# GpSimd normalises the keys by adding a negative mean instead of subtracting the mean

## The reference

```
norm_X   = layernorm(ctx, norm1_w, norm1_b)          # the keys, and the values
norm_F_L = layernorm(x + tgt2, norm2_w, norm2_b)     # the queries
attended = softmax(norm_F_L @ norm_X.T / 16) @ norm_X
h        = gelu(attended @ fc1_w.T + fc1_b)          # 4 columns
cross    = h @ fc2_w.T + fc2_b
norm_c   = layernorm(cross, norm3_w, norm3_b)
out      = norm_F_L + gamma2 * (cross + gamma1 * softmax(norm_c @ norm_c.T / 16) @ norm_c)
```

## Time and profile before

| | us |
|---|---|
| median of 3 runs | 325.54 (324.9 to 326.22) |
| the profiled execution, its own time | 324.85 |
| its span | 323.1 |

### The profile page before, as it was taken

The page is one execution under the profiler, slowest core; times in us unless marked ns, Lnnn a source line. Parts: engine busy times, 40 slices in busy tenths (PEclk is TensorE's granted clock), DMA queues, the critical chain, the costliest instruction groups (busy, mean ns, idle before and its releaser), DMA issues.

```text
span 323.1 us, 4581 instructions
## 1 busy us (share of the span) xinstructions
PE 236.0 (73%) x1614; PEld 151.0 (47%) x1614; DVE 200.4 (62%) x377; ACT 140.9 (44%) x265; POOL 157.6 (49%) x141
## 2 busy tenths in 40 slices
PE   5789971398898797878988799300678888773990
PEld 4665640377676595656767597100223222221330
DVE  6585744689765595766576433399444444427992
ACT  1253831158656375656557484400353443321220
POOL 8000199959999999999999920007000000000000
PEclk9956998589999799999999999955555555555555
DMA  7910000074314243432400000000000000000998
GB/s 234 388 63 2 1 3 1 0 231 156 134 40 144 78 133 130 132 131 78 149 35 2 1 2 0 0 0 0 2 1 0 2 0 0 2 0 1 359 365 318
DMA packets 14710, 26.79 MB, mean 83 GB/s; under 512 B 1760, under 2 KB 1760, under 8 KB 14688
## 3 DMA queue, kind: packets, MB, share of 16 engines
q1 hardware_dynamic: 14688, 26.50, 23.6%
HBM read 18.11 MB, written 8.39 MB: 82 GB/s over the span
## 4 chain that ended last, share of the span: by engine, by line
POOL 40%; PE 30%; DVE 20%; issue 4%; ACT 3%; DMA 1%; SPq 0%; DVEq 0%; ACTq 0%; POOLq 0%
POOL cN L586 23%; POOL xN L567 10%; POOL rstd L574 6%; DVE Fall L530 6%; DVE nm L485 5%; PE psum L960 5%; PE psum L833 4%; PE psum L930 3%; PE psum L790 3%; PE psum L802 2%; PE psum L779 2%; PE psum L749 2%; PE psum L813 2%; PE psum L968 1%; DVE PT L457 1%
## 5 line engine op out<-in xcount | busy, mean ns | idle before, releaser
L586 POOL TENSOR_SCALAR cN<-cN,bn,rstd 128x256 f32<-128x256 f32 x64 | 80.0, 1259 | 1.5
L833 PE MATMUL psum<-XT,Fall 128*128 128x256 f32 x256 | 62.9, 390 | 0.0
L833 PEld LDWEIGHTS psum<-XT,Fall 128*128 128x128 f32 x256 | 48.0, 198 | 5.6
L317 DVE BATCH_NORM_STATS2 bn<-xN 128x6 f32<-128x512 f32 x32 | 22.3, 699 | 28.0 <-POOL xN L567 28.0
L567 POOL TENSOR_TENSOR xN<-xN,tgt 128x512 f32<-128x512 f32 x30 | 38.1, 1274 | 1.9 <-DMA xN<-x 1.9
L682 ACT ACTIVATE PT<-psum 128x512 f32<-128x512 f32 x32 | 19.1, 597 | 43.3 <-PE psum L841 43.3
L410 DVE TENSOR_REDUCE nmax<-psum 128x2 f32<-128x512 f32 x32 | 22.0, 688 | 21.8 <-PE psum L833 21.8
L779 PE MATMUL psum<-ident,cN 128*128 128x128 f32 x128 | 20.2, 290 | 17.3 <-POOL cN L586 17.3
L333 DVE TENSOR_SCALAR xN<-xN,bn,rstd 128x256 f32<-128x256 f32 x64 | 30.0, 512 | 0.1
L669 ACT ACTIVATE Fall<-psum,par 128x512 f32<-128x512 f32 x32 | 23.4, 791 | 13.6 <-PE psum L779 13.5
L688 ACT ACTIVATE E<-psum,nmax 128x256 f32<-128x256 f32 x64 | 26.7, 471 | 5.8 <-DVE nmax L410 5.8
(11 more groups left out here) (153 smaller groups left out, 340.3 us busy)
## 6 DMA issues: line engine op xcount, KB each, us to landing
cN<-ctx SPq DMA_DIRECT2D x32, 256.0 KB, 3.0
xN<-x SPq DMA_DIRECT2D x32, 256.0 KB, 4.1
out<-Fall SPq DMA_DIRECT2D x32, 256.0 KB, 3.5
x0T<-x0t SPq DMA_DIRECT2D x1, 256.0 KB, 2.8
wqT<-wqt SPq DMA_DIRECT2D x1, 256.0 KB, 3.0
c0T<-c0t SPq DMA_DIRECT2D x1, 256.0 KB, 3.5
wkT<-wkt SPq DMA_DIRECT2D x1, 256.0 KB, 4.6
wvT<-wvt SPq DMA_DIRECT2D x1, 256.0 KB, 4.9
```

Of the source, the lines that this page charges most:

```text
L317: dve.bn_stats(bn[:, (b // 2) % 4, side, b % 2, :], src[:, b % SLOTS, :].rearrange("p (t d) -> p d t", t=NT)).then_inc(st_ok, 1)
L586: pool.tensor_scalar(own, own, stat(p, 0, m, t, 1), root_of(p, 0, m, t), ALU.subtract, ALU.mult)\
L833: last = pe.matmul(bank[SBANK1[b % 3]][:, t * N:(t + 1) * N], Fall[:, b, c, t * P:(t + 1) * P], XT[:, p % 4, c, m * N:(m + 1) * N], start= ...
```

## The change

The negative means are written to a new small array `nmean`. VectorE writes them with one more `tensor_scalar` ahead of the one that writes the variances: once for the first three pairs (12 columns), and once for each of the 13 later pairs (4 columns). GpSimd's `tensor_scalar` of L586 keeps its tile, its shape and its number, but its two operations are add and mult where they were subtract and mult, and its first pointer leads to `nmean` in place of `bn`. GpSimd has one more wait in `normal` for each batch of the later pairs. VectorE's own `normal` (L333) keeps subtract and mult.

```diff
+    nmean = sb("nmean", [P, 4, 2 * NT])
...
         def variances(p):
             sides = slice(1, 2) if p < EARLY else slice(0, 2)
             dve.wait_ge(st_ok, stats[0])
+            if p >= EARLY:
+                dve.tensor_scalar(nmean[:, p % 4, :].rearrange("p (m t) -> p m t", t=NT),
+                                  bn[:, p % 4, 0, :, :].rearrange("p m (t k) -> p m t k", t=NT)[:, :, :, 1],
+                                  -1.0, None, ALU.mult).then_inc(nmean_ok, 1)
             dve.tensor_scalar(vps[:, p % 4, sides, :]...
...
                 elif p == 2 * EARLY:
                     dve.wait_ge(st_ok, 2 * EARLY)
+                    dve.tensor_scalar(nmean[:, 0:EARLY, :].rearrange("p q (m t) -> p q m t", t=NT),
+                                      bn[:, 0:EARLY, 0, :, :].rearrange("p q m (t k) -> p q m t k", t=NT)[:, :, :, :, 1],
+                                      -1.0, None, ALU.mult).then_inc(vps_first, 1)
...
             if p < EARLY:
                 pool.wait_ge(root_first, 1)
             else:
+                pool.wait_ge(nmean_ok, p - EARLY + 1)
                 pool.wait_ge(root_ok, p + 1)
             for t in range(NT):
                 own = cN[:, b % SLOTS, t * D:(t + 1) * D]
-                pool.tensor_scalar(own, own, stat(p, 0, m, t, 1), root_of(p, 0, m, t), ALU.subtract, ALU.mult)\
+                pool.tensor_scalar(own, own, nmean[:, p % 4, NT * m + t:NT * m + t + 1], root_of(p, 0, m, t), ALU.add,
+                                   ALU.mult)\
                     .then_inc(zc_ok, 1)

         pool.wait_ge(consts, 13)
-        pool.wait_ge(vps_first, 1)
+        pool.wait_ge(vps_first, 2)
```

More of the change, by code:

```diff
@@ L173, in build @@
     y_first, y_ok, st_ok = sem("y_first"), sem("y_ok"), sem("st_ok")
-    vps_first, vps_ok, root_first, root_ok = sem("vps_first"), sem("vps_ok"), sem("root_first"), sem("root_ok")
+    nmean_ok, vps_first, vps_ok, root_first, root_ok = sem("nmean_ok"), sem("vps_first"), sem("vps_ok"), sem("root_first"), sem("root_ok")
     zc_ok, zy_ok, t_mm, evac_ok = sem("zc_ok"), sem("zy_ok"), sem("t_mm"), sem("evac_ok")
```

## The result

The changed kernel takes 297.77 us (median; 295.92 to 298.40), the kernel before 325.22 us beside it (321.41 to 326.22): a ratio of 0.9166, with a 95% interval of 0.9081 to 0.9252. The forecast was faster, 304.5 us, with a range from 302.5 up. The way is right, and the gain is larger than the range allowed. The profiled execution takes 298.40 us with a span of 296.5, against 324.85 and 323.1 before.

What follows compares the result with a forecast made beforehand. GpSimd was taken as the bound, with TensorE waiting for its normalised `cN`. Loop -16.3, first stretch -4.9, late root +0.2 gave -21.0 us, so 304.5 us; range 302.5 to 326.5.

Steps and rivals of the forecast that it cites:

- The price of the instruction: GpSimd's L586, 64 times: from 1219 ns undisturbed to 0.60 us, taken from the two-input add and subtract per element.
- The loop: From 72 to 182 us, TensorE's whole 17.3 us of waits for `cN` goes and no more; gain 16.3 us.
- the 1.0 us kept back: In the loop, an allowance of 1.0 us for new waits, such as a late maximum on VectorE.
- My window for the 7.83: One pair's period of the loop, 9.20 us long, in which TensorE was busy 7.83 us, taken as its need.
- the threshold: In the loop, GpSimd stops being the bound at (7.83 - 4.21) / 4 = 0.90 us per L586 instruction.
- The first stretch: From 41 to 61 us, twelve L586 instructions fall from 15.0 to 7.2 us; VectorE normalises earlier; gain 4.9 us.
- The collision that I had put into the range: First stretch: GpSimd's add beside VectorE's adds might cost 0.56 us; two such collisions cut the gain to 3.6 us.
- The clock behind the pause: TensorE restarts at half clock after its pause, before as after the change; costs and gives nothing.
- VectorE's instructions and GpSimd's wait: VectorE's 14 new instructions hidden in the loop, 0.4 us if GpSimd stays the bound; added wait nothing to some hundredths each.
- my bound of 0.48: Upper cost of one added VectorE instruction, from its twin L324, which ranges from 169 to 480 ns.
- rival A: In L586, add and mult cost the same as subtract and mult: 0.4 us added, 325.9 us; chance 0.31.
- +0.2: The one late root, at 72.06 us, which waits for its variances behind VectorE's new instruction: 0.2 us lost.

Runs made afterwards that it cites:

- run 1: The kernel before with only subtract changed to add in GpSimd's normalising, the pointer still leading to the statistics: 296.61 us, ratio 0.918.
- run 7: The changed kernel plus 16 GpSimd `tensor_scalar` probes of operation pairs on a scratch array before its first root: 0.56 or 1.22 us each at 256 elements.
- 3: The changed kernel with subtract and the old pointer kept for the first 12 normalisings (first three pairs), add for the others: 305.21 us.
- run 9: The changed kernel with VectorE's negative means counted into `vps_ok`, so GpSimd has one wait instead of two: 297.81 us.
- Run 10: run 9 with GpSimd's first add made to wait until VectorE has done its own two adds of `tgt2`: 296.37 us, ratio 0.9139.
- 12: The changed kernel with subtract kept in 1 of 4 normalisings: 298.67 us, ratio 0.9194.
- run 6: The changed kernel with 60 transposes of a constant filling TensorE's pause before the first xN transposes: 297.56 us, ratio 0.9186.
- 11: The changed kernel with subtract kept in 3 of 8 normalisings: 302.57 us, ratio 0.9314.
- run 2: The changed kernel with the mean written with its own sign and subtract kept, new array and added waits included: 327.12 us, ratio 1.0073.
- run 8: run 2 with VectorE's means counted into `vps_ok`, so GpSimd has one wait instead of two: 324.88 us, ratio 1.0004.

## Why the prediction was right and wrong

*The price of the instruction.* Right in its place and near in size: 0.60 us taken, 0.554 median. The reasoning held in what decides (the data are not the limit of this form, and its price can hang on its operations), and run 1 shows that nothing else matters. The way to 0.60 was luck: I scaled the two-input add, and the quick form is in truth 0.34 us and 0.83 ns per element, the rate at which two of the casts grow, (825 - 507) / 384 for L624 and L620. The GPSIMD Engine Reference of the Trainium skill (section 3.1) gives 1.03 cycles per element for a loop of at most two operations, an estimated 0.86 ns at its 1.2 GHz. That agrees with the quick pairs of run 7, and not with the others, at 3.5 ns.

*The loop: the step that failed.* I took 7.83 us of busy time as TensorE's need in a period, wrote that "the whole 17.3 us of TensorE's wait goes and no more", and kept 1.0 us of that back: 16.3. Measured: 21.4. The waits did go whole. The words "and no more" failed, because TensorE's busy time shrank as well. From its second score to its last product with `V1` (columns as in the earlier trace rows), before and after:

```profile
68.93:205.02 136.09, 116.70 (x872) 92.45 (x871) 86.21 (x181) 83.39 (x154) 116.01 (x89) 0.99 0.26 86
```

```profile
63.97:178.66 114.69, 112.59 (x873) 91.39 (x871) 89.12 (x194) 81.37 (x154) 81.10 (x89) 1.00 0.32 106
```

For the same instructions TensorE is busy 4.1 us less (116.70 - 112.59) and idle 17.3 us less (19.39 - 2.10). Two things make up the 4.1 us, and a third is the 1.0 us kept back.

First, a group of transposes that is cut by the wait counts as more busy time than a whole one. TensorE in order of time, one pair of the kernel before, and then the same group after:

```profile
133.78 0.38 PE L779 MATMUL psum<-ident,cN 128*128 128x128 f32 x2
135.53 0.88 PE L779 MATMUL psum<-ident,cN 128*128 128x128 f32 x6 [1.37 <-POOL cN L586]
136.25 1.89 PE L833 MATMUL psum<-XT,Fall 128*128 128x256 f32 x8
```

```profile
118.10 1.04 PE L789 MATMUL psum<-ident,cN 128*128 128x128 f32 x8
118.97 1.89 PE L843 MATMUL psum<-XT,Fall 128*128 128x256 f32 x8
```

From the first transpose to the score it is 2.47 us before, of which 1.37 is shown as a wait, and 0.87 us after. The difference is 1.60, so 0.23 us more goes than the wait. All 11 waits cut their group in the same way, into two and six, so over 11 that is 2.5 us.

Second, TensorE's clock fell once inside the loop of the kernel before, and not after. A window of each time, before, and one group in it:

```profile
108.00:110.00 2.00, 2.00 (x10) 1.73 (x9) 1.13 (x2) 1.47 (x2) 2.00 (x2) 0.55 0.00 0
110.00:112.00 2.00, 2.00 (x8) 1.57 (x6) 0.00 (x0) 0.00 (x0) 1.90 (x3) 0.59 0.00 0
```

```profile
108.66 3.36 PE L833 MATMUL psum<-XT,Fall 128*128 128x256 f32 x8
```

This score takes 3.36 us, the others 1.89, and the six transposes ahead of it 1.13 in place of 0.88: 1.7 us of busy time that hid a wait. The next pair, at about 117 us, is the one that has no wait for `cN`: 12 pairs, 11 waits. Before the fall TensorE had waited 1.75 us for `cN`, no longer than in other periods, where the clock stayed; what set it off isn't shown. 17.3 + 2.5 + 1.7 = 21.5, against 21.4 measured. Third, the 1.0 us that I kept back for new waits did not come: the loop takes 114.69 or 114.70 us in every run in which GpSimd is quick enough (after, 1, 3, 7, 9, 10 and 12), and 114.78 in run 6.

My window for the 7.83 was also unlucky. Pairs alternate between 7.64 and 7.20 us after (from the starts of the scores at 111.33, 118.97 and 126.17 us), and it lay on the longer kind. Runs 11 and 12 show what this means for the threshold: it is (7.42 - 4.21) / 4 = 0.80 us, not 0.90, or 0.76 if the 0.18 us of idle time behind each root is counted as well.

*The first stretch.* 4.9 forecast, 4.39 measured. The collision that I had put into the range came. Run 10, which removes it, wins back 0.24 of the missing 0.5 us; the rest is open.

*The clock behind the pause.* I took it as costing and giving nothing. It gave something: the clock is at 0.50 until 67 us before and until 61 us after, 5.3 and 3.1 us behind the restart, and the stage up to the second score is 1.17 us shorter. Run 6, with no fall there at all, is 0.70 us shorter still, so the low clock costs time in this stage. That the 1.17 us are all the clock's is argued and has no run of its own.

*VectorE's instructions and GpSimd's wait.* Costed at nothing where GpSimd is no longer the bound, and that is right for the wait (run 9) and for the instructions (run 1, which has none and is as fast). One of the 13 in the loop took 0.81 us, beyond my bound of 0.48, and VectorE had the slack for it. The price in case the cover is gone was too low: 0.4 us for both late roots and some hundredths for each wait, where the wait alone cost 0.11 us a pair, 1.45 us over the loop (run 2 against run 8). Had rival A come true, the time would have been that of run 2, 0.7% over before, and not level.

*The sum.* -21.4 for -16.3, -4.39 for -4.9, -1.17 for 0, -0.24 for 0, and 0 for +0.2: -27.2 for -21.0. The range failed at its lower end, which rested on the wait rows being all that TensorE could win. (The two terms named for it, 1.0 us in the loop and 0.5 in the first stretch, lead from 304.5 to 303.0, not to 302.5; neither holds 297.77.)

## What to carry to other kernels

The busy time of an engine that is cut by waits is not its need: take the need from a stretch where it runs without a gap, or add up undisturbed groups of one whole period, and let the range go below the sum of the wait rows. When the form of an instruction costs several times what its data cost, try other operations in it before moving the work to another engine, and price pairs, not operations. A wait that another wait already implies was free here only while its engine wasn't the bound.

## What the runs showed of the hardware that I had not expected

- GpSimd's `tensor_scalar` with two pointers has two prices by the pair of operations, 0.56 and 1.22 us for 256 elements, and add-add is among the dear ones though add-mult and mult-add are not.
- A second semaphore wait in front of one GpSimd instruction cost it 0.1 us, behind a root that it had to wait for anyway (runs 2 and 8).
- VectorE's and GpSimd's two-input adds, begun together, took 2.36 and 3.37 us where they take 1.29 and 2.49 apart. The SBUF page of the Trainium skill (Who interferes with whom) says that a VectorE instruction with two SBUF inputs contends with a GpSimd instruction that reads SBUF. The trace agrees, though not with a full exclusion: both pairs are over 3.49 us after the first began, and apart they take 3.78. The cast L619, begun 0.03 us after a two-input VectorE instruction of 2.56 us (L457), took 3.21 us where L624, of its shape, takes 0.82.
- A pause filled with idle work kept the clock at 1.00 and won 0.70 us. The clock then fell earlier at the end of the loop, as it did in two runs without the fill, and the time stayed the same. What ties the two, if anything does, is open.
